# A transformer block on one core: the first pass's token order kept to the end, the image of no group first, hats spread by three full transfers

## The chip, the cores and the metric

The kernel runs on one NeuronCore of one Trainium2 chip. The metric is the device time in microseconds of one execution, taken as the median of three runs. PE is TensorE, DVE VectorE, ACT ScalarE, POOL GpSimd, SP the engine that issues nearly all DMAs.

## What is computed

Sixteen images of 16 x 16 tokens with 96 channels in fp32 go through two blocks. Cut to what matters:

```
x = x + window_attention(ln(x))        # shifted 8x8 windows, 12 heads, position bias, cosine scores
t = x + bitlinear_mlp(ln(x))           # sign weights; clip and scale by the largest |y| of a GROUP of images:
                                       #   5 groups of 3 images; rows outside the groups get 0 (image 15)
x = t + deformable_attention(ln(t))    # q -> 3x3 grouped conv -> ln -> gelu -> offsets (tanh);
                                       #   bilinear sampling of x at the offsets; k, v; attention of 256 tokens
y = x + moe(ln(x))                     # 4 experts, top 2, hidden 384, exact gelu
```

The first line is a token-window matter: a token belongs to one of four windows of the image rolled by 4. The third needs for each token its neighbours in the image, and samples with two "hats": for every source column and row, max(0, 1 - |distance|), multiplied.

## The kernel before, in words

All 16 images stay in SBUF (`x_all`, 128 partitions x 2 tiles x 96 per image), all weights too. The work of an image is cut into some 55 pieces: names with `a_` are the window attention and the first half of the MLP, `b_`/`gam`/`w2m`/`yt`/`x2` the rest of the MLP, whose clip needs the largest value of all three images of a group, and names with `c_` the deformable attention and the experts. Here `a_` to `x2` are called the first pass, `c_` the second pass.

The order of the pieces on each engine is written out by hand-placed tables, `PLAN_PE`, `PLAN_ACT`, `PLAN_DVE`, `PLAN_POOL`, `PLAN_SP`: every piece of every image with a due time. `turns` sorts them; only the order is used, each engine runs its list in that order, and semaphores (`at(name, i)`) and the PSUM banks (`banks.take`) hold a piece back until what it needs is there. Pieces of up to four images lie beside each other. `run` calls set-up functions (the table of the position bias, sign weights) at the n-th turn of the list.

The two passes use two token orders. In the first, partition p holds a token of a window of the rolled image, in the second token 2p + t lies in partition p, tile t. So after its first pass each image goes through DRAM: `leave(i)` on SP writes it out in 12 small DMAs (6 or 12 KB), `back(i)` reads it back in one, and the second pass begins with `c_st(i)` on DVE, which waits for `x_back`. After it come `c_ln` (POOL), `c_xn` (DVE), `c_xt` (PE, two transposes), `c_xnt` (ACT, one copy of 128 x 256 into the padded planes `xpp`), `c_q`, `c_sh` (POOL), `c_conv` (PE), and the hats: `c_th` (ACT), `c_hat` (DVE), then `hout` and `hin` on SP write the hats to DRAM and read them back spread over the partitions (`hy` 768 KB and `hx` 1536 KB in one DMA), and `c_w0` to `c_w2` (DVE) multiply them for `c_sm` (PE).

At the start the position bias table is made by two matmuls (`table_1`), written to DRAM and read back by eight DMAs into `ebraw`, and turned into place by `table_2` on PE: 24 matmuls of 32 columns. All of it stands ahead of the first image's `a_xt(0)` on PE, ACT's `table_2`, `bias_exp` and `signs` ahead of `a_xnt(0)`.

Images 0 to 14 are the five groups, image 15 belongs to none.

Of the kernel before, what the change touches and what calls it, by code (L numbers as in the profile page):

```python
# [5 lines left out]
F32 = mybir.dt.float32  # L6
# [6 lines left out]
P = 128  # L13
IMAGES = 16
# [15 lines left out]
QIMG = GROUPS * GIMG  # L30
EPSQ = 1e-5
# [19 lines left out]
a_s1 18.40 37.51 54.20 70.89 87.58 108.73 125.10 148.13 168.36 190.73 214.51 240.83 281.51 311.50 363.54 409.02
a_s2 18.91 38.02 54.71 71.40 88.09 109.24 126.00 148.64 168.87 191.24 215.02 241.34 282.21 312.01 364.05 409.53
a_nm 21.66 40.77 57.46 74.15 90.84 112.38 129.65 151.83 172.01 195.23 218.16 245.33 287.83 330.47 367.88 421.40
a_stt0 22.71 41.82 58.51 75.20 91.89 113.43 130.70 152.88 173.06 197.58 224.05 246.38 296.07 343.90 371.53 424.34
a_stt1 23.52 42.63 59.32 76.01 92.70 114.24 131.51 153.69 173.87 198.39 224.86 247.19 296.88 344.71 372.34 425.15
a_stt2 24.33 43.44 60.13 76.82 94.99 115.05 133.49 154.50 174.68 200.68 225.67 248.00 297.69 345.52 373.15 425.96
a_pv0 31.51 47.97 64.66 81.35 101.94 119.50 138.94 161.57 181.51 206.38 231.37 273.03 303.39 354.53 399.94 435.07
a_pv1 32.02 48.48 65.17 81.86 102.45 120.01 139.45 162.08 182.02 206.89 231.88 273.54 303.90 355.04 400.45 435.58
a_osel 33.25 49.92 66.61 83.30 103.68 121.24 140.86 163.31 183.46 208.33 233.11 274.77 305.22 358.10 402.26 439.20
a_ont 35.15 51.84 68.53 85.22 105.98 123.40 142.78 165.61 185.38 212.63 235.48 281.96 307.03 360.13 403.63 440.57  # L60
a_proj 36.18 52.87 69.56 86.25 108.28 125.55 147.68 167.91 190.28 214.06 240.38 284.07 308.63 361.51 405.36 442.21
a_x2t 0:44.19 1:60.88 2:77.57 3:95.74 4:112.98 5:130.25 6:155.25 7:176.91 8:201.43 9:219.61 10:250.17 11:290.33 12:316.29
    13:373.90 14:432.23
a_y1 0:46.62 1:63.31 2:80.00 3:97.39 4:115.80 5:134.24 6:157.63 7:180.16 8:205.03 9:226.42 10:256.97 11:294.43 12:322.34
    13:383.45 14:436.07
gam1 2:85.47 5:141.11 8:210.36 11:300.05 14:442.66
w2m 0:98.74 1:103.93 2:106.23 3:156.28 4:163.56 5:165.86 6:222.70 7:227.77 8:233.36 9:318.94 10:323.69 11:326.36 12:458.36
    13:460.63 14:463.06
gam2 2:117.15 5:183.71 8:251.82 11:330.72 14:470.85
yt 0:121.86 1:123.80 2:124.85 3:193.92 4:195.63 5:197.33 6:261.94 7:265.97 8:267.30 9:334.28 10:335.50 11:337.50 12:479.19  # L70
    13:480.52 14:482.77
c_xt 135.59 171.40 215.72 216.77 268.75 332.25 376.82 439.45 483.82 516.55 533.17 566.78 600.39 634.00 667.61 701.03
c_q 137.54 177.16 250.42 313.41 368.13 413.76 442.88 486.39 514.07 548.60 582.21 615.82 649.43 683.02 716.44 749.86
c_conv 143.03 185.63 235.73 252.77 276.80 339.70 379.25 444.53 487.79 525.01 558.62 592.23 625.84 659.45 692.87 726.29
c_tt 155.50 215.47 246.01 267.55 289.13 370.75 431.63 476.01 512.35 547.00 580.61 614.22 647.83 680.19 713.61 747.03
c_offs 160.65 219.86 259.57 272.11 290.83 374.15 434.15 493.07 517.61 551.22 584.83 618.44 652.05 685.64 719.06 752.48
c_sm 195.88 260.49 292.20 317.49 347.19 398.49 471.05 518.53 552.14 585.75 619.36 652.97 686.56 719.98 753.40 779.78
c_kv 201.68 264.22 300.48 328.72 409.98 426.96 481.02 522.18 555.79 589.40 623.01 656.62 690.04 723.46 756.88 782.31
c_s0 208.58 269.84 321.26 353.45 416.30 441.13 495.86 529.21 562.82 596.43 630.04 663.65 697.07 730.49 762.34 794.23
c_s1 218.41 275.02 325.28 358.35 420.32 448.73 502.80 534.46 568.07 601.68 635.29 668.90 702.32 735.74 766.42 798.36  # L80
c_s2 229.77 286.48 330.92 366.80 430.06 452.97 507.60 538.83 572.44 606.05 639.66 673.27 706.69 740.11 772.00 802.94
c_q2 245.76 298.88 352.28 390.35 440.82 475.76 512.10 543.38 576.99 610.60 644.21 677.82 711.24 744.66 779.25 807.31
c_stt0 258.32 302.23 377.88 395.03 461.98 479.44 515.47 547.25 580.86 614.47 648.08 681.69 715.11 748.53 781.23 808.91
c_stt1 262.19 307.37 384.80 400.90 468.82 484.36 520.15 553.76 587.37 620.98 654.59 688.01 721.43 754.85 785.24 813.42
c_pv0 263.27 312.46 385.88 407.56 469.90 485.44 521.23 554.84 588.45 622.06 655.67 689.09 722.51 755.93 786.32 814.50
c_stt2 266.22 315.21 389.10 412.68 474.62 491.99 523.93 557.54 591.15 624.76 658.37 691.79 725.21 758.63 788.86 819.56
# [1635 lines left out]
```

## Time and profile before

| | us |
|---|---|
| median of 3 runs | 1014.95 |
| lowest, highest | 1008.29, 1016.97 |
| the profiled execution's own time | 1014.97 |
| its span, first to last instruction | 1013.1 |
| PE busy | 802.2 (79%) |
| DVE busy | 490.8 (48%) |
| ACT busy | 444.0 (44%) |
| POOL busy | 354.3 (35%) |
| mean granted TensorE clock | 0.925 |

The profiled execution lasts 1.9 us longer than its span, and its time is the median of the runs. The granted clock is 1.0 at 2.4 GHz and 0.5 at 1.2 GHz. A matmul of fp32 operands shows as two records, a transpose as one.

### The profile page before, as it was taken

How to read it: one execution, taken by the hardware profiler on the slowest of the kernel's cores; microseconds unless marked ns; L12 is line 12 of the kernel's file. 1: busy time of each engine (PE TensorE's matmuls, PEld its weight loads, DVE VectorE, ACT ScalarE, POOL GpSimd, SP SyncE). 2: the span in 40 equal slices, each digit the busy share in tenths (PEclk: the TensorE clock that was granted, in tenths of full speed). 3: DMA queues.
4: the chain of work that ended last, by engine and by line, in shares of the span. 5: the costliest groups of instructions: out<-in, count | busy, mean ns of one | idle time of the engine just before them, and what ended most of it. 6: DMA issues, size and time to landing. Idle time of an engine off the chain costs nothing.

```text
span 1013.1 us, 27125 instructions
## 1 busy us (share of the span) xinstructions
PE 802.2 (79%) x11232; PEld 622.7 (61%) x11232; DVE 490.8 (48%) x1080; ACT 444.0 (44%) x690; POOL 354.3 (35%) x866
## 2 busy tenths in 40 slices
PE   3466776276828875897799898499999999999998
PEld 2345555164616753675777666377777787776766
DVE  3244454263428616674536733455664465465411
ACT  0233352152305431752585483145435444553573
POOL 3335445353424504631512221224423322331233
PEclk9999888597959996998899998799999899999999
DMA  7000000004003033510130400442144044404000
GB/s 218 23 2 4 3 3 7 20 2 103 6 20 85 21 80 90 126 44 19 40 69 6 102 4 25 114 103 68 41 105 106 13 95 106 99 22 91 6 6 12
DMA packets 23450, 53.45 MB, mean 53 GB/s; under 512 B 9552, under 2 KB 18080, under 8 KB 21280
## 3 DMA queue, kind: packets, MB, share of 16 engines
q1 hardware_dynamic: 22752, 51.47, 21.3%
q8 instruction: 90, 1.47, 0.6%
q10 hardware_dynamic: 576, 0.25, 0.1%
q14 instruction: 32, 0.26, 0.1%
HBM read 45.40 MB, written 6.30 MB: 51 GB/s over the span
## 4 chain that ended last, share of the span: by engine, by line
PE 38%; DMA 7%; issue 4%; DVE 4%; SPq 3%; POOL 3%; ACT 2%; POOLq 0%; ACTq 0%; DVEq 0%
PE ps L1214 35%; DMA hx<-hat_scratch 5%; SPq L473 3%; PE ps L1221 1%; DVE nmx L936 1%; DMA hat_scratch<-hat 1%; ACT prob L1169 1%; DVE hat L917 0%; DVE hat L916 0%; DMA x_all<-x_scratch 0%; ACT L1169 0%; PE ps L1476 0%; PE ps L1270 0%; PE ps L1506 0%; ACT L1196 0%
## 5 line engine op out<-in xcount | busy, mean ns | idle before, releaser
L936 DVE TENSOR_REDUCE nmx<-ps 128x4 f32<-128x1024 f32 x96 | 114.4, 1220 | 50.2 <-PE ps L1214 49.8
L1196 ACT ACTIVATE hidden<-ps 128x512 f32<-128x512 f32 x96 | 57.2, 597 | 142.2 <-PE ps L1214 141.9
L1214 PE MATMUL ps<-turned_x,we 128*128 128x256 f32 x384 | 104.6, 397 | 0.0
L1214 PE MATMUL ps<-we,hidden 128*128 128x96 f32 x768 | 103.4, 287 | 0.7 <-ACT hidden L1196 0.7
L1214 PEld LDWEIGHTS ps<-we,hidden 128*128 128x128 f32 x768 | 96.9, 200 | 11.0 <-issue 7.1
L1169 ACT ACTIVATE prob<-ps 128x1024 f32<-128x1024 f32 x96 | 93.5, 1025 | 16.3 <-PE ps L1214 15.4
L545 POOL TENSOR_SCALAR veps_c<-mv_c 128x2 f32<-128x2 f32 x32 | 9.3, 290 | 235.5 <-DVE mv_c L711 235.2
L1214 PEld LDWEIGHTS ps<-turned_x,we 128*128 128x128 f32 x384 | 67.4, 194 | 17.0 <-issue 7.6
L1214 PE MATMUL ps<-wconv,xpp 128*128 128x96 f32 x576 | 71.6, 286 | 4.2 <-POOL xpp L631 3.7
L1214 PE MATMUL ps<-u_turned 32*64 32x64 f32 x3072 | 52.9, 238 | 27.1 <-DVE nmx L936 17.7
L1214 PEld LDWEIGHTS ps<-wconv,xpp 128*128 128x128 f32 x576 | 69.8, 202 | 7.1 <-POOL xpp L631 4.1
L925 DVE TENSOR_TENSOR wprod<-hx,hy 128x1024 f32<-128x1024 f32 x48 | 59.1, 1237 | 27.9 <-DMA hx<-hat_scratch 27.8
L1214 PEld LDWEIGHTS ps<-u_turned 32*64 32x64 f32 x3072 | 48.0, 138 | 32.0 <-issue 30.5
L1214 PE MATMUL ps<-q2t,ckt 32*128 32x256 f32 x768 | 57.1, 411 | 2.9 <-ACT u_turned L1090 1.4
L1214 PE MATMUL ps<-ckt,cqt 32*128 32x256 f32 x768 | 56.9, 411 | 2.8 <-ACT prob L1169 1.5
L708 DVE BATCH_NORM_STATS2 stats_c<-x_all 128x6 f32<-128x96 f32 x64 | 13.4, 252 | 84.4 <-DMA x_all<-x_scratch 83.3
L1270 PE MATMUL ps<-ident,stk 128*128 128x128 f32 x192 | 33.6, 322 | 20.7 <-DVE stk L773 15.9
L1214 PE MATMUL ps<-prob,vc 128*32 128x256 f32 x768 | 49.7, 384 | 0.1
L1214 PEld LDWEIGHTS ps<-ckt,cqt 32*128 32x128 f32 x768 | 36.1, 189 | 16.6 <-issue 10.2
L1214 PE MATMUL ps<-u_turned,va 64*32 64x64 f32 x1536 | 20.5, 241 | 31.8 <-issue 20.4
L1214 PEld LDWEIGHTS ps<-q2t,ckt 32*128 32x128 f32 x768 | 36.1, 189 | 14.5 <-issue 8.7
L545 POOL TENSOR_SCALAR veps_a<-mv_a 128x2 f32<-128x2 f32 x31 | 10.6, 341 | 90.3 <-DVE mv_a L711 88.9
(230 smaller groups left out, 1616.4 us busy)
## 6 DMA issues: line engine op xcount, KB each, us to landing
hx<-hat_scratch SPq DMA_DIRECT2D x16, 1536.0 KB, 12.7
hy<-hat_scratch SPq DMA_DIRECT2D x16, 768.0 KB, 5.9
hat_scratch<-hat SPq DMA_DIRECT2D x32, 96.0 KB, 1.9
x_scratch<-x_all SPq DMA_DIRECT2D x128, 6.0 KB
x_all<-in_x SPq DMA_DIRECT2D x4, 384.0 KB, 4.3
x_all<-x_scratch SPq DMA_DIRECT2D x16, 96.0 KB, 1.9
out<-u_hid SPq DMA_DIRECT2D x16, 96.0 KB, 1.7
x_scratch<-x_all SPq DMA_DIRECT2D x64, 12.0 KB
```

The lines of the kernel that those rows point to most:

```text
L473: sp.dma_start(image[a0:a0 + rows, c0:c0 + 4, :], x_all[p0:p0 + 4 * rows, i, t, :]).then_inc(landed("x2_out", i), 16)
L545: own.link(g.tensor_scalar(veps[key][:], mv[key][:, r, :, 1], eps, None, ALU.add))
L708: own.mark(v.bn_stats(stats[key][:, t, :], src[t]))
L925: v.tensor_tensor(wprod[:, :, 2 * j:2 * j + 2, :].rearrange("p t g n -> p t (g n)"), hx[:].rearrange("p (t n) -> p t n", t=TILES)[:, :, n ...
L936: v.tensor_reduce(dst, src, AX.X, ALU.max, negate=True).then_inc(sem("c_mx"), 1)
L1169: a.activation(prob[:, k % 4, :], flat(4 + 2 * (k % 2), 1024), ACT.Exp, scale=float(HD) ** -0.5).then_inc(sem("c_exp"), 1)
L1196: a.activation(hidden[:, 2 * k:2 * k + 2, :].rearrange("p m n -> p (m n)"), ps[:, k % 2, :], ACT.Gelu).then_inc(sem("c_h"), 1)
L1214: return m.matmul(o, l, r, start=start, stop=stop)
L1221: ins = m.transpose(ps[:, bank, cols(t)], src[:, t, :], ident[:])
L1270: ins = m.transpose(ps[:, t, cols(g)], stk[:, t, x, cols(g)], ident[:])
```

## The change

- The token order of the first pass is kept through the second (and the output; the host puts the tokens in place). `leave`, `back`, the scratch tensor and the semaphores `x2_out` and `x_back` are gone. `c_st(i)` waits for `x2` (`b_x2`) or, for the image of no group, for `a_x1`.
- Windows are held row by row (a partition is window row, window column of a tile), so `hx` is read as two DMAs, one for each tile of 8 columns, beside `hy`: three DMAs of 768 KB each over all 128 partitions.
- `c_xt` transposes twice as often: once for `c_q` (copied by `c_xnt` into a new tile `cxt`) and once in image order, from which the new piece `c_xp` on ACT makes the two planes of `xpp` by four copies with strided reads. `c_sh` waits for `c_xp`.
- The image of no group is image 0 of the kernel's list; groups are images 1 to 15 (`fed`, `group`, `ends`, `FIRST`).
- Set-up functions are tied to pieces. On PE `table_2` has 12 matmuls of 64 columns and stands ahead of `a_tq(0)`, a new `sums` ahead of `a_tk(0)`; on ACT `table_2` ahead of `a_qt(0)`, `bias_exp` ahead of `a_nmt(0)`, `signs` ahead of `a_ot(0)`; on DVE the `weights_*` ahead of `a_ss`, `a_qn`, `a_mx` of image 0. POOL's `late` goes from the second piece of its list to ahead of `a_ln(2)`. Weights are loaded in other portions: `LW` (wqt, wconv, be2; 880 KB) goes ahead of the table's round trip, `L5` behind.
- All five tables are written anew, with image 0's second pass beginning beside the first pass of image 1. In the old lists 380 of PE's 870 pieces stand behind the last `yt`, in the new one 228.

```
-            def leave(i):
-                w("b_x2" if fed(i) else "a_x1", i)
...
-                            sp.dma_start(image[a0:a0 + rows, c0:c0 + 4, :], x_all[p0:p0 + 4 * rows, i, t, :]).then_inc(landed("x2_out", i), 16)
-            def back(i):
-                sp.wait_ge(*at("x2_out", i))
-                w("x_back", i - 1)
-                sp.dma_start(x_all[:, i], x2_dram[TOK * i:TOK * i + TOK, :].rearrange("(p t) k -> p t k", t=TILES)).then_inc(sem("x_back"), 16)
...
-                xrow = bass.AP(d.tensor, d[1].offset, [[0, SIDE], [2 * DG * TOK, 8], [1, 2 * DG * TOK]])
-                sp.dma_start(hy[:], yrow).then_inc(landed("hat_in", i), 16)
-                sp.dma_start(hx[:], xrow).then_inc(landed("hat_in", i), 16)
+                rows = bass.AP(d.tensor, d[0].offset, [[line, SIDE], [0, 8], [1, line]])
+                sp.dma_start(hy[:], rows).then_inc(landed("hat_in", i), 16)
+                for t in range(TILES):
+                    cols = bass.AP(d.tensor, d[1].offset + 8 * t * line, [[0, SIDE], [line, 8], [1, line]])
+                    sp.dma_start(hx[:, t, :], cols).then_inc(landed("hat_in", i), 16)
...
             def c_st(i):
-                dve.wait_ge(*at("x_back", i))
+                w("b_x2" if fed(i) else "a_x1", i)
...
         def fed(i):
-            return i < QIMG
+            return i >= FIRST
+
+        def group(i):
+            return (i - FIRST) // GIMG
...
             def c_xnt(i):
                 act.wait_ge(*at("c_xt", i))
-                w("c_q", i - 2)
+                w("c_q", i - 1)
+                a.copy(cxt[:], ps[:, 2, 0:TOK]).then_inc(sem("c_xnt"), 1)
+
+            def c_xp(i):
+                act.wait_ge(*at("c_xt", i))
                 w("c_conv", i - 2)
-                a.copy(xpp[:, i % 2, 1:3, 8:8 + P], ps[:, 2, 0:TOK].rearrange("p (a n) -> p a n", a=2)).then_inc(sem("c_xnt"), 1)
+                half, low = SIDE // 2, SHIFT // 2
+                turned_rows = ps[:, 2, TOK:2 * TOK].rearrange("p (r n a) -> p a r n", a=2, n=half)
+                planes = xpp[:, i % 2, 1:3, 8:8 + P].rearrange("p a (r n) -> p a r n", n=half)
+                for r0, r1, rt in ((0, SIDE - SHIFT, SHIFT), (SIDE - SHIFT, SIDE, 0)):
+                    for n0, n1, nt_ in ((0, half - low, low), (half - low, half, 0)):
+                        a.copy(planes[:, :, rt:rt + r1 - r0, nt_:nt_ + n1 - n0], turned_rows[:, :, r0:r1, n0:n1]).then_inc(sem("c_xp"), 1)
...
                 pe.wait_ge(sem("bt_in"), 16 * 8)
                 for b in range(2):
-                    for ch in range(2):
-                        src = ebraw[:, 6 * b:6 * b + 6, :].rearrange("p h (r c) -> p h r c", c=15)[:, :, :, 4 * ch:4 * ch + 4]
-                        for h in range(6):
-                            ins = mm(ps[:, 6 + b, WIN * h + 32 * ch:WIN * h + 32 * ch + 32], flip[:], src[:, h])
+                    src = ebraw[:, 6 * b:6 * b + 6, :].rearrange("p h (r c) -> p h r c", c=15)[:, :, :, 0:8]
+                    for h in range(6):
+                        ins = mm(ps[:, 6 + b, cols(h, WIN)], flip[:], src[:, h])
...
             def c_xt(i):
...
-                banks.take([2], "c_xnt", i)
-                turn(2, pads["c_xn"][:, i % 2]).then_inc(sem("c_xt"), 1)
+                banks.take([2], "c_xp", i)
+                src = pads["c_xn"][:, i % 2]
+                turn(2, src)
+                for t in range(TILES):
+                    o = ps[:, 2, TOK:2 * TOK].rearrange("p (r n) -> p r n", r=SIDE)[:, :, 8 * t:8 * t + 8]
+                    ins = m.transpose(o, src[:, t, :], ident[:])
+                ins.then_inc(sem("c_xt"), 1)
...
-            run(pieces, PLAN_PE, {0: [table_1, table_2]})
+            run(pieces, PLAN_PE, {("a_xt", 0): [table_1], ("a_tk", 0): [sums], ("a_tq", 0): [table_2]})
```

The first forty places of PE's order, before and after:

```
before: a_xt:0 a_qkv:0 a_xt:1 a_tk:0 a_tq:0 a_s0..2:0 a_qkv:1 a_xt:2 a_nm:0 a_stt0..2:0 a_pv0..1:0 a_tk:1 a_osel:0 a_tq:1 a_ont:0 a_proj:0
        a_s0..2:1 a_qkv:2 a_xt:3 a_nm:1 a_stt0..2:1 a_x2t:0 a_y1:0 a_pv0..1:1 a_tk:2 a_osel:1
after:  a_xt:0 a_qkv:0 a_xt:1 a_tk:0 a_tq:0 a_s0..2:0 a_qkv:1 a_xt:2 a_nm:0 a_stt0..2:0 a_pv0..1:0 a_tk:1 a_osel:0 a_ont:0 a_tq:1 a_proj:0
        a_s0..2:1 a_qkv:2 a_xt:3 a_nm:1 a_stt0..2:1 c_xt:0 c_q:0 a_pv0..1:1 a_tk:2 a_osel:1 c_conv:0
```

## Rows read from the trace of the kernel before

**Rows 1.** The page: busy time of each engine

```profile
PE 802.2 (79%) x11232; PEld 622.7 (61%) x11232; DVE 490.8 (48%) x1080; ACT 444.0 (44%) x690; POOL 354.3 (35%) x866
```

**Rows 2.** Windows (A:B us, busy time, clock, DMA share, GB/s) over PE's five longest gaps

```profile
178.10:197.00 18.90, 0.04 (x1) 0.00 (x0) 3.31 (x18) 0.99 (x2) 4.06 (x8) 0.58 0.09 25
...
641.20:654.20 13.00, 0.04 (x1) 0.08 (x1) 2.24 (x3) 0.66 (x1) 0.00 (x0) 0.66 0.74 164
sum 75.50, PE 0.24 PEld 0.11 DVE 16.05 ACT 4.70 POOL 11.71; mean PE 0.05 PEld 0.02 DVE 3.21 ACT 0.94 POOL 2.34
```

**Rows 3.** Waits of DVE: us in total, times, longest

```profile
DVE stats_c L708 <- DMA x_all<-x_scratch: 83.3, 7, 20.0
DVE stk L773 <- POOL rn L571: 50.2, 16, 6.2
```

**Rows 4.** Timeline of SP around two bursts

```profile
167.12 16.23 SPq L473 DMA_DIRECT2D x_scratch<-x_all  x24
183.40 0.44 SPq L478 DMA_DIRECT2D x_all<-x_scratch  x1
...
636.56 0.92 SPq L484 DMA_DIRECT2D hat_scratch<-hat  x2
```

**Rows 5.** Timeline of DVE, the wait for the hats that those issues bring

```profile
651.96 1.23 DVE L925 TENSOR_TENSOR wprod<-hx,hy 128x1024 f32<-128x1024 f32 x1 [13.52 <-DMA hx<-hat_scratch]
```

**Rows 6.** Windows over the 17 half-speed stretches, sums: five behind gaps, twelve others

```profile
sum 81.90, PE 25.69 PEld 19.37 DVE 31.35 ACT 3.49 POOL 24.25; mean PE 5.14 PEld 3.87 DVE 6.27 ACT 0.70 POOL 4.85
...
sum 68.00, PE 54.97 PEld 46.33 DVE 29.18 ACT 15.47 POOL 20.53; mean PE 4.58 PEld 3.86 DVE 2.43 ACT 1.29 POOL 1.71
```

**Rows 7.** Timeline of all engines, the start

```profile
9.21 0.51 POOL L551 TENSOR_TENSOR pad_a_xn<-pad_a_xn,rstd_a 128x192 f32<-128x192 f32 x1
...
19.36 10.45 PE L1214 MATMUL ps<-hx,wprod 64*128 64x32 f32 x48 [4.75 <-DMA hx<-bt_scratch]
...
34.90 0.35 ACT L1048 COPY turned_a_xn<-ps 128x256 f32<-128x256 f32 x1
...
49.47 1.76 PE L1214 MATMUL ps<-u_turned 32*64 32x64 f32 x96 [0.98 <-ACT u_turned L1080]
```

**Rows 8.** Groups by line: PE's transposes of c_xt, ACT's copy of c_xnt

```profile
L1221 PE MATMUL ps<-ident,pad_c_xn 128*128 128x128 f32 x32 | 7.1, 308 | 19.8 <-DVE pad_c_xn L896 18.9 <-ACT xpp L1132 0.6 <-DVE x_all L884 0.4
...
L1132 ACT COPY xpp<-ps 128x256 f32<-128x256 f32 x16 | 6.0, 374 | 35.0 <-PE ps L1221 35.0
```

**Rows 9.** ACT: the experts' gelus by line; timeline around a table load

```profile
L1196 ACT ACTIVATE hidden<-ps 128x512 f32<-128x512 f32 x96 | 57.2, 597 | 142.2 <-PE ps L1214 141.9
...
939.97 1.94 ACT L1169 ACTIVATE prob<-ps 128x1024 f32<-128x1024 f32 x2 [1.32 <-PE ps L1214]
941.93 1.28 ACT L1196 ACT_TABLE_LOAD   x1
```

**Rows 10.** Windows over stages of the span

```profile
98.00:178.10 80.10, 55.53 (x1420) 45.23 (x1420) 37.88 (x89) 31.29 (x58) 40.06 (x89) 0.85 0.02 4
...
233.00:240.00 7.00, 0.36 (x14) 0.28 (x7) 0.55 (x4) 0.00 (x0) 0.00 (x0) 0.70 1.08 233
298.00:372.90 74.90, 67.36 (x1232) 52.69 (x1232) 44.77 (x100) 37.93 (x60) 28.22 (x65) 0.96 0.18 42
390.60:459.00 68.40, 60.68 (x1006) 44.77 (x1006) 48.37 (x104) 38.67 (x61) 34.63 (x78) 0.96 0.33 77
466.20:555.80 89.60, 81.15 (x1370) 64.57 (x1374) 46.47 (x87) 53.10 (x72) 26.70 (x60) 0.93 0.15 35
...
700.00:860.00 160.00, 156.79 (x1453) 121.22 (x1453) 88.90 (x171) 73.41 (x111) 46.53 (x113) 0.98 0.37 84
934.00:1013.10 79.10, 71.27 (x597) 54.96 (x591) 20.77 (x54) 43.84 (x59) 26.66 (x76) 0.98 0.02 8
```

**Rows 11.** Timeline of PE, one piece of two following images

```profile
835.12 1.10 PE L1214 MATMUL ps<-turned_tn,woffp 128*128 128x256 f32 x4
...
868.91 1.10 PE L1214 MATMUL ps<-turned_tn,woffp 128*128 128x256 f32 x4
```

More of the change, by code:

```diff
@@ L51 @@
[L51 to L55, printed above, removed]
@@ L69 @@
[L69 to L74, printed above, removed]
@@ L208 @@
[L208 to L211 removed]
+a_ln 1.15 4.20 7.25 21.33 40.70 60.86 82.03 100.38 129.16 181.36 206.74 266.18 290.77 309.86 410.29 495.26
@@ L498, in store @@
                 sp.dma_start(out[TOK * i:TOK * i + TOK, :].rearrange("(p t) k -> p t k", t=TILES), acc[:, i % 2]).then_inc(landed("done", i), 16)
-            run(dict(leave=leave, back=back, hout=hout, hin=hin, store=store), PLAN_SP, {})
+            run(dict(hout=hout, hin=hin, store=store), PLAN_SP, {})
             for i in range(IMAGES - RING, IMAGES):
@@ L510, in _ @@
             own.mark(g.memset(neghalf[:], -0.5))
+            own.mark(g.memset(w2s[:].rearrange("p m n -> p (m n)"), 0.0))
             own.mark(g.memset(nst[:].rearrange("p t n -> p (t n)"), 0.0))
@@ L532, in late @@
             def late():
-                own.mark(g.memset(w2s[:].rearrange("p m n -> p (m n)"), 0.0))
                 own.mark(g.memset(nmx[:].rearrange("p t n -> p (t n)"), 0.0))
@@ L694, in _ @@
             run(dict(a_ln=a_ln, a_nw=a_nw, a_ln2=a_ln2, dg1=dg1, lim1=lim1, dg2=dg2, lim2=lim2, c_ln=c_ln, c_xz=c_xz, c_sh=c_sh, c_cr=c_cr,
-                     c_ln3=c_ln3, c_rank=c_rank, c_acc=c_acc), PLAN_POOL, {1: [late]})
+                     c_ln3=c_ln3, c_rank=c_rank, c_acc=c_acc), PLAN_POOL, {("a_ln", 2): [late]})
         @block.vector
@@ L997, in _ @@
             scale_in()
-            run(pieces, PLAN_DVE, {1: [weights_1, weights_2, weights_3, bias_8]})
+            run(pieces, PLAN_DVE, {("a_ss", 0): [weights_1], ("a_qn", 0): [weights_2], ("a_mx", 0): [weights_3, bias_8]})
         @block.scalar
@@ L1204, in _ @@
             scale_in()
-            run(pieces, PLAN_ACT, {0: [table_1, table_2, bias_exp, signs]})
+            run(pieces, PLAN_ACT, {("a_xnt", 0): [table_1], ("a_qt", 0): [table_2], ("a_nmt", 0): [bias_exp], ("a_ot", 0): [signs]})
         @block.tensor
@@ L1371, in gamma @@
             def gamma(n, i):
-                w(f"b_dg{n}", i // GIMG)
-                banks.take([2], f"b_gr{n}", i // GIMG)
+                w(f"b_dg{n}", group(i))
+                banks.take([2], f"b_gr{n}", group(i))
                 mm(ps[:, 2, 0:P], onesm[:], diag[:, n]).then_inc(sem(f"b_gam{n}"), 1)
@@ L1616, in _constants, with _order, _places @@
     return c
+def _order():
+    return list(range(QIMG, IMAGES)) + list(range(QIMG))
+def _places():
+    import numpy as np
+    tile, part = np.arange(TILES), np.arange(P)
+    win, j = part // WIN, part % WIN
+    r, col = j // 8, j % 8
+    K = (SHIFT + 8 * tile[None, :] + col[:, None]) % SIDE
+    R = np.broadcast_to(((SHIFT + 8 * win + r) % SIDE)[:, None], K.shape)
+    return R, K
 def _layout(a):
```

431 lines of the change are left out of this document (222 added, 209 removed).

## The prediction

> **What bounds the kernel now.** I read the busy times first, then windows over PE's gaps, then who made DVE and SP wait, then windows over whole stages. PE is busy 802.2 of 1013.1 us and no other engine above half of the span [rows 1], so PE paces the kernel and 211 us are its gaps. The reader is to see three things. First, five gaps hold 75.5 us of them, and in these all engines stand: of 75.5 us DVE works 16, POOL 12, ACT 5 [rows 2]. Second, they come from the way through DRAM between the passes. When a group of three images is done, SP issues 12 small DMAs for each; 24 take 16.2 us before the first read back is issued [rows 4]. DVE, whose next piece is `c_st`, waits for it: 83.3 us in seven waits [rows 3], with the first pass's pieces queued behind. The gap at 641 is the same cause one step on: `hout`, queued on SP behind such a burst, is issued at 636.56 [rows 4], and DVE waits 13.5 us for the hats [rows 5]. Third, density: PE is busy 69% of the time while only first passes run, 90% where both passes lie beside each other (209.2 of 232.9 us in three stretches), 98% where only second passes run [rows 10].
>
> The clock adds to it. In 17 stretches it is at 0.5 (1.2 GHz), 149.9 us in all, in which PE is busy 80.7 us [rows 6]; at 2.4 GHz that would be 40.3 less, so the work is 761.9 us. The five stretches that begin in or at the end of the five gaps carry 25.7 us of busy time, 12.8 us of excess [rows 6].
>
> **The change part by part.**
>
> *The way through DRAM goes.* DVE's `c_st` then waits for DVE's own `x2` (or `a_x1`), already done when it comes up. Off go 75.5 us of gaps [rows 2] and 12.8 us of half speed behind them [rows 6]: -88.3. SP loses 192 issues of 0.68 us (16.23/24 [rows 4]), so `hout` and `hin` are issued when due. In the gaps nearly nothing runs on any engine, so no work of theirs has to be placed elsewhere. The bounds: all of it (-88.3), or only half, if other waits are just behind (-44). I take all and a term for late waits below.
>
> *Start.* The first window scores run at 49.47 [rows 7]. New chain: the first normalized tile is ready at 9.72, 0.4 later with the `w2s` memset now ahead of it: `a_xt(0)` at 10.2 instead of 29.7. From these transposes to the scores are 15.3 us without ACT's and PE's table work (34.90 to 49.47 and 0.7 of transposes [rows 7]). Into this chain come: on POOL `late` and `a_ln(2)` ahead of `a_nw(0)`, by my count of their durations 3.4 us beyond what ACT and DVE take anyway (0 to 6); on PE `table_2` ahead of `a_tq(0)`. Its 48 records take 10.45 us, 0.22 each at half speed [rows 7]; 24 of twice the columns take 5.2 if the weights set the pace, 10.4 if the columns do. Sum 10.2 + 15.3 + 3.4 + 5.2 = 34.1, so -15.4 (-10 to -18). `LW` (880 KB) ahead of the table's round trip delays it: at the 233 GB/s of full DMA engines [rows 10] by 3.8 us, at half that rate by 7.6, from 19.4 to 27.0 at worst, when PE comes to it. The exp and signs on ACT and DVE fall beside it: nothing on the path; were they bare, 1.5 us.
>
> *`c_xt` and `c_xp`.* 32 more transposes on PE at 0.14 (pipelined) to 0.31 us [rows 8]: +4.5 to +9.9, I take +5, since they are issued back to back. ACT has four strided copies for one piece more; one of 128 x 256 takes 0.37 [rows 8], so 0.8 to 1.5 us an image, 13 to 24 in all on an engine busy 44% [rows 1]. `c_conv` waits longer by that, with `c_q` and others beside it: nothing, at most +10.
>
> *Hats.* The same 2.3 MB in three DMAs; one issue more, 0.6 us on SP's path, 16 times, beside other work. The last wait of a bad case was 13.5 us [rows 5]. I counted in the written orders what DVE does between `c_hat(i)` and `c_w0(i)`, by durations of the trace: median 8 us of work before, 12.7 after. So the wait shrinks rather than grows: 0, bounds -15 and +10.
>
> *The new order.* It has a price on ACT. Counting changes between the exp and the gelu family in ACT's list gives 70 table loads before and 92 after. One takes 1.28 us and starts 0.02 us after the activation before it ends [rows 9]. 22 x 1.28 = 28.2 us on ACT. ACT has room, but an exp or gelu that a PE piece waits for comes 1.3 later: half on the path, +14 (0 to +28).
>
> The Trainium skill, ScalarE: Activation LUTs, section "What ACT_TABLE_LOAD costs", adds a drain of about 1380 ns to each switch. By it the switches would cost 2.66 x 22 = 58.5 us, half of it 29, and an estimate that takes it ends 15 later; the trace shows no drain of this size.
>
> *Late waits.* With the large gaps gone, small ones are next: the newton steps on POOL that DVE waits for 16 times, 50.2 us in all [rows 3], and 7.0 us at 233 with all engines idle and the DMA engines at 1.08 [rows 10]. With second-pass pieces among POOL's steps some grow: +8, from nothing to +48.
>
> **Sum.** 1013.1 - 88.3 - 15.4 + 5 + 14 + 8 = 936.4 of span, and 1.9 around it: 938. The profiled execution (1014.97) is the median of the runs, so no shift.
>
> A second way, by density. Work at full speed 761.9 + 5 - 2.6 = 764. Start 34 us with 14 of work. Until image 1's second pass begins PE has six first passes and most of image 0's second, about 76 us, at 0.72 (between first pass alone and mixed): 106. A second pass is 33.8 us (835.12 to 868.91 [rows 11]); 228 pieces behind the last `yt` are 6.5 images, 220 us: 150 at 0.97 and the last 79 us as now (71 busy [rows 10]), 234. The rest, 454, at the mixed stretches' density at full speed (198 of 232.9, 0.85): 534. Together 908; with table loads and late waits 930 of span, 932. The two agree within 6 us; I stay with 938, since the new order keeps PE's mixed stretch for 640 pieces instead of 490.
>
> **Rivals.**
> - *Tables and waits hidden* (0.20). The loads fall where ACT waits for PE anyway: it waits 142.2 us before the experts' gelus alone [rows 9]. Then 1013.1 - 88.3 - 15.4 + 5 + 1.9 = 916. Against it: over 96 gelus that is 1.5 us each, hardly more than one load.
> - *Tables on the path whole* (0.10). Every switch delays PE: 938 + 14 = 952, and with bare switches at a higher price up to 966. The skill's drain, named above, points this way; the row speaks against it.
> - *POOL's newton late* (0.12). `a_nw` is 13 small steps, now queued behind `c_ln3`, `c_rank` and `c_acc` of other images. If DVE's 16 waits of 3.1 us double, and the order was tight there, 938 + 50 = 988. Against it: POOL is 35% busy.
> - *Slower: PE runs dry in hat transfers* (0.04). At 233 PE stops inside a piece, with no wait in the code, all engines idle and the DMA engines full with the hats [rows 10]; I take it for instructions that come late through the same DMA engines. Such a gap costs 6.6 us and, as the five gaps do in the mean (12.8/5), 2.6 of half speed behind it. Before, one of 16 transfers does it. It decides from 9 more on: 938 + 9 x 9.2 = 1021; all 15 give 1076. Three full transfers in denser traffic could. The Trainium skill, Runtime: NRT & Kernel Launch, section "Instruction fetch mechanics", calls the cost of such refills mostly hidden; the row at 233 is an exception to it.
> - *Nothing gained* (0.04). If the stalls' place is taken whole by waits of the new order, since image groups close as late as before: 1013.1 - 15.4 + 5 + 1.9 = 1005 or more. Against it: after the change no engine waits for SP at a group's end.
>
> **How the numbers follow.** The forecast, 938 with its own range 922 to 952, has 0.50. The rest as above. The range 905 to 985 takes in hidden tables (916 and 10 for the unknown of the start and of the hats) and most of the newton case and leaves out slower and nothing-gained. About 1% (10 us) is what a measurement of this kernel can tell from no change. Faster by over 1%, below 1005: 0.91. Same: 0.04. Slower: 0.05.
>
> **What would show it.** Right: DVE's waits for `x_all<-x_scratch` are gone; no PE gap above 8 us behind 50 us; first scores at 32 to 38; busy share of PE 83% or more, with mean clock 0.94 or above; ACT busy near 490 (28 of tables, 16 of copies more); PE busy near 790. Wrong: gaps of PE of 10 us and more in another place, DVE waiting longer for POOL's `rn` or for `hx`, or an order so loose that many gaps of 1 to 3 us add up; then the density of the mixed stretch, 0.85, is the step that failed.

## The result, and the profile after

The changed kernel takes **943.26 us**, the median of 4 runs (941.2 to 944.65), against 1015.15 us of the kernel before on the same chip: ratio 0.9302, 95% interval 0.9254 to 0.9350, so 7% faster. The forecast was 938, with a range of 905 to 985. Of the kernel after, the profiled execution took 941.2 us, its span is 939.4 us and its mean TensorE clock 0.945. A run more than 1.5% above the fastest of its kernel counts as slow and enters no median here; of the changed kernels this touches only two of the six runs with one image copy, below.

The page of the kernel after: busy time of each engine.

```profile
span 939.4 us, 27041 instructions
...
PE 804.0 (86%) x11240; PEld 625.5 (67%) x11240; DVE 482.4 (51%) x1080; ACT 479.0 (51%) x776; POOL 341.1 (36%) x866
```

Against [rows 1], PE's busy time has hardly moved, 802.2 to 804.0. The span is 73.7 us shorter (1013.1 - 939.4), and all of this is time in which PE stood: 210.9 us before, 135.4 after, 75.5 less. This is, to the tenth, what the five long gaps held [rows 2]. That the two agree so well is partly chance, as the experiments show.

Waits of DVE after, the longest (engine and line that waited, what it waited for, us in total, times, longest):

```profile
DVE u_hid L980 <- PE ps L1220: 46.7, 19, 9.9
DVE stk L770 <- POOL rn L568: 45.4, 11, 7.3
DVE nmx L933 <- PE ps L1220: 44.4, 29, 6.2
```

The wait of 83.3 us for the trip through DRAM that heads [rows 3] is gone. The wait for POOL's `rn` is nearly as before: 45.4 us in 11 times, against 50.2 in 16. DVE now waits mostly for PE, which is what a kernel paced by PE should show.

Waits of PE after, the same columns:

```profile
PE ps L1220 <- issue: 24.5, 12, 5.2
PE ps L1220 <- ACT prob L1175: 9.0, 8, 1.7
PE ps L1220 <- DVE nmx L933: 7.5, 11, 1.8
```

No gap is longer than 6.3 us (the first load), and behind 50 us none is longer than 4.2. In their place stand more of 1 to 2 us: by the starts and ends of PE's records, 29 gaps with 41.2 us in all, where there were 21 with 28.2.

Timeline of PE at the start of the kernel after (start, us, instructions, idle before and what ended it):

```profile
9.87 0.66 PE L1227 MATMUL ps<-ident,pad_a_xn 128*128 128x128 f32 x2 [0.94 <-POOL pad_a_xn L548]
...
24.07 5.38 PE L1220 MATMUL ps<-hy,wprod 64*128 64x64 f32 x24
...
32.17 1.12 PE L1220 MATMUL ps<-u_turned 32*64 32x64 f32 x54 [1.25 <-ACT u_turned L1077]
```

The first window scores run at 32.17, against 49.47 in [rows 7]; the bias products, 24 records of twice the columns, take 5.4 us in place of 10.45.

Windows over the 16 half-speed stretches after (PEclk 0.50, which is 1.2 GHz), first, last and sum:

```profile
45.10:55.40 10.30, 7.19 (x181) 6.47 (x183) 3.63 (x10) 2.34 (x4) 0.00 (x0) 0.50 0.01 2
...
792.60:796.10 3.50, 3.50 (x22) 1.83 (x18) 0.00 (x0) 3.03 (x8) 2.68 (x12) 0.51 0.02 5
sum 102.40, PE 87.92 PEld 74.03 DVE 46.16 ACT 28.89 POOL 29.82; mean PE 5.50 PEld 4.63 DVE 2.89 ACT 1.81 POOL 1.86
```

This is the first surprise. The half-speed time fell from 149.9 us [rows 6] to 102.4, but PE is busy in 87.9 us of it, against 80.7. Half of that is the excess over full speed: 44.0 now, 40.3 before. The five stretches behind the long gaps, which held 12.8 of the excess, are gone, but the others hold 44.0 where they held 27.5. The work at full speed is 804.0 - 44.0 = 760.0, before 761.9.

One thing is missing from this reckoning in every kernel: the start. The view shows a clock of 1.00 there, but the trace has no clock record before 54.9 us (41.7 in the changed kernel), and the same four matmuls take nearly twice as long as later. From the kernel before:

```profile
0.00:54.90 54.90, 24.86 (x180) 19.81 (x180) 15.61 (x48) 11.03 (x27) 18.77 (x64) 1.00 0.39 111
```

```profile
35.30 2.29 PE L1214 MATMUL ps<-wqkv,turned_a_xn 128*128 128x288 f32 x4 [4.87 <-ACT turned_a_xn L1048]
...
72.51 1.21 PE L1214 MATMUL ps<-wqkv,turned_a_xn 128*128 128x288 f32 x4 [1.12 <-ACT wconv L1053]
```

So the start probably ran at half speed too, as the prediction took it for the bias products. Half of PE's busy time there would be a further excess of 12.4 us before and 11.2 after, by estimate; no comparison below moves by more than 2.6 us through it.

### The profile page after: what moved, and what is told of

It reads as the page before. It is cut to its first block, busy times and chain, and to the rows that moved or that the text cites. A ratio compares the mean times of both kernels' runs of the same rounds, so it can differ in the third digit from the quotient of the medians.

```text
span 939.4 us, 27041 instructions
## 1 busy us (share of the span) xinstructions
PE 804.0 (86%) x11240; PEld 625.5 (67%) x11240; DVE 482.4 (51%) x1080; ACT 479.0 (51%) x776; POOL 341.1 (36%) x866
## 4 chain that ended last, share of the span: by engine, by line
PE 54%; issue 6%; DVE 5%; ACT 5%; POOL 4%; POOLq 0%; DVEq 0%; ACTq 0%
PE ps L1220 50%; DVE nmx L933 2%; ACT prob L1175 2%; PE ps L1227 1%; PE ps L1277 1%; DVE wprod L922 1%; ACT L1202 1%; ACT L1175 1%; POOL rstd_c L543 0%; ACT hidden L1202 0%; PE ps L1488 0%; DVE u_hid L980 0%; POOL nt L565 0%; POOL rn L567 0%; ACT L1195 0%
## 5 line engine op out<-in xcount | busy, mean ns | idle before, releaser
L1175 ACT ACTIVATE prob<-ps 128x1024 f32<-128x1024 f32 x96 | 94.7, 1023 | 28.1 <-PE ps L1220 27.5
L1220 PE MATMUL ps<-we,hidden 128*128 128x96 f32 x768 | 101.1, 284 | 4.2 <-issue 2.9
L1220 PEld LDWEIGHTS ps<-we,hidden 128*128 128x128 f32 x768 | 94.0, 197 | 12.7 <-issue 9.9
L1220 PEld LDWEIGHTS ps<-u_turned 32*64 32x64 f32 x3072 | 50.7, 146 | 13.1 <-issue 12.8
L1220 PEld LDWEIGHTS ps<-q2t,ckt 32*128 32x128 f32 x768 | 37.2, 193 | 27.2 <-issue 12.6
L1220 PE MATMUL ps<-prob,vc 128*32 128x256 f32 x768 | 52.3, 384 | 0.5 <-ACT prob L1175 0.5
L980 DVE TENSOR_TENSOR u_hid<-ps,gates 128x384 f32<-128x384 f32 x32 | 17.8, 555 | 46.7 <-PE ps L1220 46.7
L1087 ACT ACTIVATE u_turned<-ps 128x768 f32<-128x768 f32 x32 | 24.2, 808 | 28.9 <-PE ps L1220 28.9
L542 POOL TENSOR_SCALAR veps_c<-mv_c 128x2 f32<-128x2 f32 x32 | 10.2, 318 | 76.5 <-DVE mv_c L708 75.9
```

Of the source, the lines that this page charges most:

```text
L542: own.link(g.tensor_scalar(veps[key][:], mv[key][:, r, :, 1], eps, None, ALU.add))
L980: v.tensor_tensor(yg[:, h], src, gates[:, i % 2, :, 2 * h:2 * h + 2].to_broadcast([P, TILES, 2, C]), ALU.mult).then_inc(sem("c_ym"), 1)
L1087: a.activation(prob_a[:, 2 * b:2 * b + 2], ps[:, 4 + 2 * b:6 + 2 * b, 0:TILES * HG * WIN], ACT.Exp).then_inc(sem("a_exp"), 1)
L1175: a.activation(prob[:, k % 4, :], flat(4 + 2 * (k % 2), 1024), ACT.Exp, scale=float(HD) ** -0.5).then_inc(sem("c_exp"), 1)
L1220: return m.matmul(o, l, r, start=start, stop=stop)
```

## The experiments

Times are medians; the ratio is against the kernel before on the same chip (1013 to 1017 us), with its 95% interval.

**The trip alone taken away.** The kernel before, with `leave` and `back` dropped from SP's pieces and this in `c_st`:

```
-                dve.wait_ge(*at("x_back", i))
+                w("b_x2" if fed(i) else "a_x1", i)
```

> The kernel before with only the trip through DRAM taken away: the second pass reads the first pass's rows in x as they lie, after the same piece that wrote them; order tables, set-up and hat transfers are those of before. It leaves out the change of token order between the passes, so the second pass works on other neighbourhoods. Theory A (the trip's gaps on TensorE and the half-speed time behind them are the whole of the gain, 88.3 us): 1015 - 88 = 927, range 920 to 935, and the gaps over 8 us are gone. Theory A without its clock term (the gaps of 75.5 us go, half-speed time stays): 1015 - 75.5 = 939.5, range 936 to 945. Rival B (the gain needs the new order of the pieces; behind the trip other waits stand ready and take its place): 965 or more.

Measured: **939.69 us** (937.03 to 941.05), ratio 0.9249 (0.9217 to 0.9281), 77 us less. Windows over its half-speed stretches, sum, and over the stage where only second passes run:

```profile
sum 97.70, PE 77.95 PEld 62.97 DVE 47.25 ACT 25.43 POOL 39.75; mean PE 4.87 PEld 3.94 DVE 2.95 ACT 1.59 POOL 2.48
```

```profile
540.00:700.00 160.00, 157.80 (x1487) 121.45 (x1489) 88.26 (x183) 82.04 (x120) 52.79 (x122) 0.99 0.30 70
700.00:860.00 160.00, 156.12 (x1452) 118.89 (x1445) 90.11 (x166) 74.80 (x114) 46.07 (x117) 0.99 0.35 82
```

Rival B falls: no other wait stood behind the trip. Theory A holds without its clock term. The excess at half speed is 39.0 us (half of 77.95), 1.3 less than before where 12.8 had been forecast. Of the 77.9 us by which the profiled span is shorter, 74.2 are idle time of PE (210.9 against 136.7), 1.3 are excess and 2.3 work. This one edit gives at least as much as the whole change did (72 us): its four runs all lie below the four of the changed kernel, though the intervals of the two ratios just overlap. So all else in the change, taken together, gives nothing or costs.

**The set-up put back ahead** in the changed kernel (PE shown; ACT, DVE and POOL alike):

```
-            run(pieces, PLAN_PE, {("a_xt", 0): [table_1], ("a_tk", 0): [sums], ("a_tq", 0): [table_2]})
+            run(pieces, PLAN_PE, {("a_xt", 0): [table_1, sums, table_2]})
```

> The changed kernel with the set-up put back ahead as before: on TensorE the bias products and sums run before the first attention's later pieces, on ScalarE all set-up at the first copy, on VectorE before the second image's statistics. Nothing is left out. Theory A (the start is on the path in full, since TensorE is the bound): 943 + 15 to 17 = 958 to 960. Rival (the first stage has other slack that takes it up, so the earlier first scores were worth nothing): 943 to 947.

Measured: **956.99 us** (951.92 to 962.91), ratio 0.9417 (0.9368 to 0.9466). That is 13.7 us more, a little under the 15 to 17 expected, with intervals that don't overlap those of the changed kernel. The first scores run at 47.0 in it, 14.8 us later than at 32.17, so the start is on the path nearly in full.

With the trip worth 77 and the start 14, the change should have come to about 925. It is at 943, so some 18 us are lost elsewhere. The next runs look for them.

**No table loads.** In both kernels, `ACT.Gelu` becomes `ACT.Tanh` in all three places:

```
-                a.activation(hidden[:, 2 * k:2 * k + 2, :].rearrange("p m n -> p (m n)"), ps[:, k % 2, :], ACT.Gelu).then_inc(sem("c_h"), 1)
+                a.activation(hidden[:, 2 * k:2 * k + 2, :].rearrange("p m n -> p (m n)"), ps[:, k % 2, :], ACT.Tanh).then_inc(sem("c_h"), 1)
```

> The changed kernel with every Gelu replaced by Tanh, whose table holds Exp too: some 90 table loads of 1.28 us leave ScalarE (115 us of its time). It leaves out the true Gelu. Theory A (half of a table load is on the path, as in the forecast's sum): 943 - 58 = 885, and 14 us more gained than by the same replacement in the kernel before. Rival B (table loads are hidden beside TensorE): 935 to 943. Rival C (they are on the path in full): 943 - 115 = 828.

> The kernel before with the same replacement of Gelu by Tanh (it leaves out the true Gelu): some 69 table loads of 1.28 us (88 us) leave ScalarE. Theory A (half on the path): 1015 - 44 = 971. Rival B (hidden): 1007 to 1015. Rival C (in full): 927. The gain here beside that of the changed kernel tells what the 22 extra loads cost: 14 us more there by theory A, 0 to 3 by B, 28 by C.

Measured: changed kernel **930.27 us** (925.31 to 934.14), ratio 0.9149 (0.9104 to 0.9195), 13 us less; kernel before **1013.39 us**, ratio 0.9964 (0.9946 to 0.9982), 3.4 us less. The pages of the two, first the changed kernel without loads, then the kernel before without them:

```profile
PE 794.1 (86%) x11240; PEld 617.4 (67%) x11240; DVE 483.6 (52%) x1080; ACT 361.5 (39%) x685; POOL 342.6 (37%) x866
```

```profile
PE 803.3 (80%) x11232; PEld 625.3 (62%) x11232; DVE 489.8 (48%) x1080; ACT 354.6 (35%) x621; POOL 357.7 (35%) x866
```

ACT's instructions fall by 91 (776 to 685) and by 69 (690 to 621), so one load is left in each, and ACT loses 117.5 and 89.4 us of busy time. Of these 117.5 us only 13 come out as time, 0.14 us for a load of 1.28. Theory A (half) falls, and rival C with it; B (hidden) is nearer, though 13 us are not nothing. In the kernel before only 3.4 us come out. Its long gaps don't hide the loads, for of 70 only one begins in them; but the same five gaps measure 78.2 us in the run without loads, 2.7 more than before, so part of what is saved ahead of a gap is waited away in it. The difference of the two gains, 9.6 us, is therefore no clean price of the 22 extra loads. The run after next gives a better one.

**The old order with the new operations.** The changed kernel's code, its order tables replaced by those of the kernel before (`leave` and `back` left out, `c_xp` placed behind `c_xnt`), `FIRST = 0`, a second query buffer so that this order can run, and `wqt` laid into `wprod`, where it is needed in the set-up only, to make room:

```
-FIRST = IMAGES - QIMG
+FIRST = 0
...
-        cxt = sb("cxt", [P, TOK])
+        cxt = sb("cxt", [P, 2, TOK])
...
-c_xt 44.61 146.84 149.82 183.57 281.54 314.03 390.37 419.95 459.99 531.10 568.45 619.93 662.19 686.42 740.45 774.46
+c_xt 135.59 171.40 215.72 216.77 268.75 332.25 376.82 439.45 483.82 516.55 533.17 566.78 600.39 634.00 667.61 701.03
```

> The changed kernel (no trip, token order kept, hats by three transfers, one query copy and four image copies, set-up tied to pieces) run in the order of pieces of the kernel before, with groups of images 0 to 14 and the last image alone; the query's buffer is doubled so that this order can run. Nothing is left out. From the trip's measured 77 and the start's measured 14: 1017 - 77 - 14 = 926, and the new transposes and copies on top. Theory A (the new order, with its 22 table loads, eats 12 us or more of the gain; the operations cost 0 to 5): 926 to 931, so faster than the changed kernel. Rival B (the 17 us that are missing lie in the operations, and the order is free): 940 to 945.

Measured: **916.74 us** (911.78 to 918.87), ratio 0.9024 (0.8994 to 0.9055). With nothing left out it beats both: 26.5 us under the changed kernel, and 9 us under even theory A. The new order of pieces costs more than was missing. The doubled buffer isn't the reason: with the single one ACT's copy into `cxt` waits for PE's reads of it only twice, 2.2 us in all. Its page:

```profile
PE 786.7 (86%) x11240; PEld 612.9 (67%) x11240; DVE 493.4 (54%) x1080; ACT 450.9 (49%) x754; POOL 354.8 (39%) x866
```

Windows of this kernel over its half-speed stretches, sum, and over the stage with second passes only (its last `yt` ends at 535):

```profile
sum 74.00, PE 54.49 PEld 47.39 DVE 31.26 ACT 19.16 POOL 21.52; mean PE 3.89 PEld 3.39 DVE 2.23 ACT 1.37 POOL 1.54
```

```profile
540.00:700.00 160.00, 158.68 (x1489) 123.10 (x1488) 94.88 (x190) 77.33 (x135) 50.72 (x118) 1.00 0.35 84
700.00:860.00 160.00, 157.29 (x1489) 119.37 (x1492) 87.15 (x166) 83.18 (x130) 49.47 (x128) 1.00 0.29 68
```

And the changed kernel over five windows that cover the span (its last `yt` ends at 695.7):

```profile
0.00:300.00 300.00, 220.16 (x4159) 174.11 (x4160) 148.03 (x349) 123.45 (x226) 124.49 (x316) 0.89 0.23 56
300.00:540.00 240.00, 216.83 (x3087) 166.70 (x3085) 138.75 (x330) 135.41 (x221) 98.51 (x257) 0.96 0.19 46
540.00:700.00 160.00, 149.22 (x2051) 118.71 (x2052) 87.95 (x183) 90.65 (x141) 42.95 (x111) 0.97 0.25 60
700.00:880.00 180.00, 167.36 (x1549) 125.88 (x1547) 91.46 (x173) 98.14 (x148) 54.65 (x126) 0.99 0.29 68
880.00:939.40 59.40, 50.46 (x403) 40.13 (x401) 16.25 (x47) 31.34 (x42) 20.50 (x58) 1.00 0.03 8
```

The two spans differ by 22.5 us (the medians by 26.5: the profiled run is the fastest of four there, and the second slowest of six here). By the same reckoning as above, 16.8 of it is half speed (an excess of 44.0 against 27.2), 5.2 idle time of PE (135.4 against 130.2), and 0.5 work. That the clocks differ is no accident of the profiled runs: the four runs of the changed kernel have mean clocks of 0.929 to 0.945, the six of the old order 0.948 to 0.962. How much time the lower clock costs is less sure, for the 16.8 is a reckoning and no run changed the clock alone. Within one kernel the clock moves further than the time does: the changed kernel took 941.2 us at 0.945 and 944.4 at 0.929, the old order 915.3 at 0.948 and 918.2 at 0.962. Of the 16.8 us, 7.7 lie in the first 300 us, 2.1 in the next 240 and 6.9 behind 540, where the old order has no half-speed stretch but the last 2.5 us, with PE idle. The idle time lies elsewhere, too. Where only second passes run, the old order keeps PE busy in 316.0 of 320 us (98.7%), the new one in 167.4 of 180 (93%). The new order had bought some time early, as it was meant to: up to 540 PE stands 103.0 us in it, in the old order 119.0 (300 - 205.97 and 240 - 215.06 in the same windows).

What a late gap of the new order looks like: timeline of the changed kernel at 711.

```profile
711.86 0.60 ACT L1202 ACTIVATE hidden<-ps 128x512 f32<-128x512 f32 x1 [0.71 <-PE ps L1220]
711.89 1.22 DVE L922 TENSOR_TENSOR wprod<-hx,hy 128x1024 f32<-128x1024 f32 x1
...
712.48 1.28 ACT L1195 ACT_TABLE_LOAD   x1
...
713.77 0.21 ACT L1195 ACTIVATE sc<-sc 128x8 f32<-128x8 f32 x1
...
714.00 1.28 ACT L1202 ACT_TABLE_LOAD   x1
...
714.01 0.16 DVE L965 TENSOR_REDUCE scm<-sc 128x2 f32<-128x8 f32 x1 [0.29 <-ACT sc L1195]
...
714.84 0.95 DVE L938 TENSOR_TENSOR q2t<-cqt,ps 128x768 f32<-128x768 f32 x1 [0.26 <-issue]
...
715.85 1.15 PE L1220 MATMUL ps<-q2t,ckt 32*128 32x256 f32 x16 [1.57 <-DVE q2t L938]
```

Within 2.8 us ACT loads a table twice for one small exp of 0.21 us. PE's next scores wait for `q2t`. Ahead of `q2t` in DVE's list stand the gate steps, and the first of them waits for that small exp; PE had the transposed `nmx` ready from 712.95 on. 1.57 us of idle PE come out. The load looks like the cause, but it is the smaller part of it. The same place in the changed kernel without table loads:

```profile
705.90 1.15 PE L1220 MATMUL ps<-q2t,ckt 32*128 32x256 f32 x16 [1.19 <-DVE q2t L938]
```

Without any load the gap is still 1.19 us, so the load makes 0.4 us of it and the place of `q2t` in DVE's list the rest.

**The old order without table loads:** the kernel of the last experiment with the same `ACT.Tanh`.

> The same old order of pieces with every Gelu replaced by Tanh, so that the table loads go (it leaves out the true Gelu). The changed kernel without them took 930. Theory A (the 22 extra table loads are what the new order costs): the two orders are now equal, 926 to 932, and the loads of the old order cost 0 to 3. Rival B (the new order has other waits too): 915 to 922, 10 us under the changed kernel without tables.

Measured: **908.04 us** (904.68 to 909.75), ratio 0.8940 (0.8908 to 0.8972), 8.7 us less than with them. Here both kernels have the same operations. The loads cost 13.0 us in the new order (91 of them) and 8.7 in the old (69), so the 22 extra ones are worth 4.3 us by the medians, 7 by the ratios; with runs that scatter over 5 to 9 us this is a rough figure. Without any load the orders still lie 22 us apart. Theory A (the loads are what the new order costs) falls; rival B holds, and at twice the size that it gave. Most of the order's price is in other waits and in the lower clock that comes with them; which of the moved pieces make it, no run separates.

**One image copy for four** in the changed kernel:

```
-                for r0, r1, rt in ((0, SIDE - SHIFT, SHIFT), (SIDE - SHIFT, SIDE, 0)):
-                    for n0, n1, nt_ in ((0, half - low, low), (half - low, half, 0)):
-                        a.copy(planes[:, :, rt:rt + r1 - r0, nt_:nt_ + n1 - n0], turned_rows[:, :, r0:r1, n0:n1]).then_inc(sem("c_xp"), 1)
+                a.copy(planes[:, :, 0:SIDE, 0:half], turned_rows[:, :, 0:SIDE, 0:half]).then_inc(sem("c_xp"), 1)
```

> The changed kernel with one image copy on ScalarE in place of four that put the tokens where they belong (it leaves out the restoring of the token order in the image that the convolution reads). It takes 0.6 us of ScalarE away for each image, 10 us in all. Theory A (hidden beside TensorE): 941 to 944. Rival (on the path, since the convolution waits for the copies): 933 to 937.

Measured: **940.1 us** (932.68 to 946.01, four runs; two more took 948.81 and 949.84), ratio 0.9261 (0.9204 to 0.9318). That is 3 us below the changed kernel, 1 below the range for hidden copies and 3 above the rival's. With this scatter it decides nothing finer than that the copies cost at most a few us. The edit also took less from ACT than expected, 3.1 us of busy time (479.0 to 475.9) instead of 10: the 64 copies last 16.2 us by their records, but these overlap and cover 9.3 us, and the 16 single ones cover 6.3.

**Two hat transfers for three** in the changed kernel:

```
-                for t in range(TILES):
-                    cols = bass.AP(d.tensor, d[1].offset + 8 * t * line, [[0, SIDE], [line, 8], [1, line]])
-                    sp.dma_start(hx[:, t, :], cols).then_inc(landed("hat_in", i), 16)
+                cols = bass.AP(d.tensor, d[1].offset, [[0, SIDE], [2 * line, 8], [1, 2 * line]])
+                sp.dma_start(hx[:].rearrange("p t n -> p (t n)"), cols).then_inc(landed("hat_in", i), 16)
```

> The changed kernel with the x-hats fetched by one transfer of pairs of rows, as before, in place of two transfers of single rows: two transfers to an image in place of three, the same bytes (it leaves out the right rows of the x-hats for the second tile). Theory A (the third transfer is hidden: no wait of VectorE for the hats stands in the trace): 941 to 945. Rival (its 0.6 us of issue and the shared engines delay the hats and the stores): 935 to 938.

Measured: **946.84 us** (939.99 to 951.77), ratio 0.9332 (0.9297 to 0.9368): no gain from the transfer taken away. It is 2 us above even theory A's range, with an interval that takes in that of the changed kernel. The hats' third transfer costs nothing that can be measured here.

**The old order with the set-up ahead:** the old order's kernel with the four `run` lines of the second experiment.

> The changed kernel's operations in the old order of pieces (917) with the set-up put back ahead on all engines. Nothing is left out. It has the order and the set-up of the run without the trip (940) and the changed kernel's operations. Theory A (the start is worth 14 in either order, and the operations bring the rest): 931, range 928 to 934, so 9 us under the run without the trip. Rival B (the operations are worth nothing; in the old order the earlier start is worth 23, through the clock): 938 to 942.

Measured: **932.3 us** (925.63 to 935.71), ratio 0.9188 (0.9152 to 0.9224). The start is worth 15.6 us in this order, 13.7 in the new one. Beside the run without the trip (939.7; the same order and set-up, the old operations) it lies 7 us lower, as theory A has it, so all the new operations together cost nothing and seem to give a little; the intervals of the two ratios just touch. The sum of its half-speed windows, for comparison with the run without the trip:

```profile
sum 68.40, PE 50.60 PEld 44.09 DVE 29.65 ACT 17.95 POOL 22.58; mean PE 3.89 PEld 3.39 DVE 2.28 ACT 1.38 POOL 1.74
```

Its excess is 25.3 us where that run has 39.0, with the same work (759.7 and 759.6) and 3.9 us more idle time, so in the profiled runs this, too, is the clock. Between 161.9 and 182.4 us the run without the trip has one half-speed stretch with 15.9 us of busy time; here there are two of 6.9 us in the same place, with 3.7 and 6.1. Why the clock came back sooner isn't settled: the profiled run is among the fastest of its six, whose clocks go from 0.948 to 0.963, those of the run without the trip go from 0.948 (its profiled run) to 0.953, and no run separates the new operations from each other.

## Why the prediction was right, point by point

The sum in measured terms, from run to run: 1016.8 - 77.1 (trip) - 7.4 (operations, in the old order) - 15.6 (start) + 26.5 (new order, table loads in it) = 943.3. It closes by itself, since each term is the difference of two runs. The forecast was 1015 - 88.3 + 5 - 15.4 + 14 + 8 = 938. The total is right, and the mechanism (the trip's gaps and the start) too. That it came within 5 us is partly luck: the trip was taken 11 us too large, the operations 12 us too dear, and these two cancel. The 22 for loads and late waits were 4 too few, and wrongly divided.

- **The trip** (-88.3): its gaps were read rightly. 75.5 us stood in [rows 2], 77 came. The **12.8 us of half speed behind them was mis-sized**: 1.3 came in the run without the trip. The step took the excess at every stretch that begins behind a long gap for the gap's doing. But PE works at half speed in other places as well: the excess outside those five was 27.5 us before and is 39.0 in the run without the trip. Each of its 15 half-speed stretches begins inside a gap of PE of 1.2 to 7.5 us or within 3 us of its end.
- **The start** (-15.4): scores at 34.1 were forecast, 32.17 came. The bias products took 5.4 where 5.2 was reckoned for the case that the weights set the pace. Worth 13.7 to 15.6 us, so the term holds.
- **Transposes and copies** (+5): nothing, or below. The 64 transposes, 32 of them new, have records of 0.27 to 0.29 us and cover 10.1 us where 32 covered 7.1, so +3.0. Yet PE's work at full speed fell from 761.9 to 760.0: the bias products' saving (5 of 10.45 us), which the term left to the start, paid for them. ACT's copies cost at most a few us.
- **Hats** (0): right. DVE never waits for them in the changed kernel; before, it waited 27.8 us in 8 times.
- **Table loads** (+14): the count was right (70 and 92 in the traces). The share on the path was not: not half of a load but 0.14 of 1.28 us, and 4 to 7 us for the 22. The drain of about 1380 ns that the Trainium skill names (ScalarE: Activation LUTs, "What ACT_TABLE_LOAD costs") would have made it dearer still. In the run without loads ACT's busy time fell by 1.29 us for each load taken away, and in the timeline above a load begins 0.02 us after the activation before it.
- **Late waits** (+8): waits came, and more than forecast: about 20 us, 5 of them idle time against the old order and the rest half speed by the reckoning. It wasn't the POOL steps that I named: DVE waits 45.4 us for `rn` here and 53.1 in the old order. PE waits longer for `prob` (9.0 us, 3.0 in the old order), `nmx` (7.5, 2.7) and POOL's `diag` (7.5, 1.0), and less for `stk` (5.0, 17.3). Tables and waits were given 22 together, and the new order costs 26.
- **Rivals.** Hidden tables (916): not here. The same change in the old order gives 916.7, but that is a coincidence of numbers, since 8.7 us of loads are still in it. Newton late (988): DVE's wait for `rn` fell in total, from 50.2 to 45.4. PE dry in hat transfers: three such stops for one before, but 10.8 us in all against 6.6 (see below), so it was no 9 times 9.2. Nothing gained: excluded by the result and by the first experiment.
- **The marks.** No DVE wait for the trip, no PE gap over 8 us, scores within 32 to 38, PE share 86%, clock 0.945: all as said. ACT came to 479 for 490 (its records overlap, so 16 us of copies add less to the busy time). PE's busy time was to fall to 790; it stayed at 804, and this was the mark of the failed clock term. The old order has 787.

The second way, by density, divided the span into stages. Windows of the changed kernel over three of them: from 34 us to image 1's second pass, from there to the last `yt`, and from there to the last 79 us:

```profile
34.00:171.20 137.20, 94.63 (x2186) 74.83 (x2186) 67.83 (x154) 51.32 (x97) 63.84 (x145) 0.84 0.09 21
171.20:695.70 524.50, 470.59 (x6924) 367.78 (x6925) 291.73 (x655) 286.55 (x468) 182.23 (x473) 0.95 0.22 52
695.70:860.40 164.70, 152.28 (x1397) 116.68 (x1396) 86.65 (x172) 84.72 (x132) 50.29 (x123) 0.99 0.34 80
```

Less their excess (16.6, 25.6 and 1.7 us), the densities are 0.57, 0.85 and 0.91, where 0.72, 0.85 and 0.97 were taken. So the first stage failed most: its 78 us of work, 76 by the forecast, took 137 us, not 106. The third cost 10 us more than its 155. The mixed stretch, which the prediction named as the step to fail, held at 0.85, and it was shorter than the 534 us reckoned. That this way came to 932 is luck, too: the 22 us of loads and waits, added on top, stood in for the first stage.

## What to carry to other kernels

A round trip that stops every engine gives back its gap, once it goes; the half speed behind it was no second gain here, where gaps of 1 to 7 us stayed in other places. When a change brings an operation and a new order together, run the new operations in the old order: here the operations (the trip away among them) and the earlier start were worth 100 us, and the new order took 26 of them back, which no view of the changed kernel alone would have told. And an order that fills the idle start can pay with the dense end: compare the busy share of both stages, and the half-speed time beside the idle time, since the first differed more than the second between these two orders. And before a load or a transfer is blamed for a gap, look at the same place in the run without it.

## What was not expected of the hardware

- A table load of 1.28 us costs 0.13 to 0.14 us of time in either order here by the medians (0.17 by the ratios of the new order), on an engine that is half busy. Even a kernel with 92 of them loses only 1.4% by them.
- By the reckoning the clock cost more than the waits: between the orders, PE's idle time differs by 5.2 us and its excess at half speed by 16.8. The half-speed stretches of the changed kernel are 3.4, 6.8 or 10.2 us long (to 0.1), with the engine busy for 86% of them. Each of the 16 begins inside a gap of PE of 1.2 to 5.2 us or within 3 us of its end; so do the 13 of the old order ahead of its idle end. But only 17 of the 34 gaps of 1.2 us and more in the changed kernel have such a stretch at them, and what sets these apart isn't shown.
- PE still stops between two matmuls of one piece, with no wait in the code, as at 233 before [rows 10]: at 104.0, 213.3 and 363.6, for 3.9, 4.0 and 2.9 us, each 8 to 10 us after the reading back of hats was issued. The old order has three such stops, too, with 14.9 us. Windows of the changed kernel over two of them:

```profile
213.30:217.30 4.00, 0.02 (x1) 0.00 (x0) 1.57 (x2) 1.10 (x2) 0.82 (x2) 0.81 0.32 72
104.00:108.00 4.00, 0.16 (x9) 0.16 (x16) 0.67 (x4) 0.00 (x0) 3.84 (x4) 0.82 0.90 202
```

The one at 104 has the DMA share at 0.90 and both PE and its weight loads idle, like that at 233. The one at 213 has a share of 0.32, so full DMA engines are not the only reason. What PE waits for in such gaps was not tried.

- Not every gap that ends in "issue" is of this kind. Timeline of the changed kernel at its longest behind the first load, 5.2 us at 42.0:

```profile
44.77 0.56 DVE L770 TENSOR_TENSOR stk<-qk,rn 128x384 f32<-128x384 f32 x1 [6.18 <-POOL rn L568]
...
45.26 1.83 DVE L787 TENSOR_TENSOR u_turned<-u_turned,biast 128x768 f32<-128x768 f32 x2
...
47.19 1.11 PE L1220 MATMUL ps<-u_turned,va 64*32 64x64 f32 x60 [5.22 <-issue]
```

PE starts 0.1 us after DVE has ended the `u_turned` that it reads, and that piece stood in DVE's list behind one that waited 6.18 us for POOL's `rn`. The 3.6 us at 87.8 look the same, down to the 6.18. So these two are the prediction's newton steps; the old order has a like gap at 41.0, of 6.2 us, so they are no part of the new order's price.
